# A gated cross-attention and expert kernel on one core: rank sums in a bank of their own, first expert products ahead of a permutation, stores and splits reordered

## The chip, the cores and the metric

The kernel runs on one core of a Trainium2 chip. Its engines work side by side, each through its own queue of instructions: TensorE (PE in the rows) multiplies matrices, VectorE (DVE) and ScalarE (ACT) work element by element and may read the accumulators of TensorE, GpSimd (POOL) works element by element and issues gathers, SyncE (SP) issues most other transfers. They wait for one another through semaphores that the kernel sets and awaits by hand. The metric is the device time of one execution in microseconds.

## What is computed

Two layers on 2048 tokens of width 256, in float32. A layer is a cross-attention block and a feed-forward block, each scaled by the tanh of a gate and added to its input; the first feed-forward block picks 2 of 16 experts for each token.

```python
x = x + tanh(g_xattn[0]) * L0_xattn(layernorm(x), ctx, ctx, ...)   # softmax(q k^T) v over 64 keys, by batch
x = x + tanh(g_ffn[0])   * L0_ffn(layernorm(x), gate_w, w1, w3, w2)
x = x + tanh(g_xattn[1]) * L1_xattn(layernorm(x), ctx, W, b)       # x W1^T + mean over the keys of ctx W2^T + b
x = x + tanh(g_ffn[1])   * L1_ffn(layernorm(x), ...)               # ternary weights, 256 -> 1024 -> 1024 -> 1024 -> 256

def L0_ffn(h, gate_w, w1, w3, w2):
    scores = softmax(h @ gate_w); w, idx = top_k(scores, 2); w = w / sum(w)
    y = sum over the two picked e of  w_e * (silu(h w1[e]) * (h w3[e])) w2[e]
    return y + h
```

## The kernel before

Tokens are handled in tiles of 128 and groups of four tiles: NG = 4 groups. The work has four stages. First comes a short setup. The **attention stage** (some 15 to 60 us) takes the groups one after another: transposes of X (`columns`), scores, softmax, attention (`attend`), the logits of the 16 experts, the two largest of them (`two_largest` on VectorE), and the **rank** of each token among those that picked the same expert (`ranks` on TensorE, `rank_picked` and `row_place` on VectorE). Then the **permutation**: the normed rows of all tokens (`xb`) are stored to a buffer in memory (`xb_dram`), and a product of one-hot matrices gives, for each of the NBLK = 47 blocks of 128 places, the rows to gather (`perm`); the first 16 blocks belong to experts 0 to 15, the other 31 (NREST) to whichever experts have more than 128 rows. The **block stage** (some 70 to 155 us) does for each block: gather 128 rows (GpSimd, L648), transpose them (`turns`, L1831), round to a high part (ScalarE, `high_turned`) and a low rest (VectorE, `low`), multiply with the expert's first matrices (`gate_up`, L1594 to L1596), silu and product, `down`, copy out (`yb`) and store to `ys_dram`. The last stage, four groups of the dense feed-forward network, runs from some 158 us to the end.

Every product of float32 values in the block stage uses a high and a low part of each operand. The experts' weights are loaded to six buffers ES; ScalarE writes the high part EH of an expert (`split_high`, L1363), GpSimd the low part EL of experts 0 to 12 in two halves of 384 columns (`split_low`, L587), VectorE that of experts 13 to 15 in the block stage (`expert_low`). These splits are placed in the gaps of the attention stage.

All order is written by hand. What matters here:

- On VectorE, `rank_picked(g)` (L850) waits not only for the ranks of its group but also for the logits of the next group (`pe_lg`, L856), since the ranks of group g lie in the bank of scores of group g+1.
- The last group's normed rows are made half by ScalarE (`rows_normed`, L1410), half by VectorE (`rows_normed` at L877), both from rstd and -mean*rstd, which GpSimd makes one after the other (`factors2`, L545 to L555).
- On SyncE the stores of `xb` stand behind a fill of `ys_dram` (L452), which keeps unused rows finite. GpSimd starts the gathers when `act_eh` says that all 16 EH are there (L619), both store semaphores are reached and `perm` is written.
- TensorE runs fillers (`keep_clock`, products of the identity whose result nobody reads) where it would wait.

## Time and profile before

| | us |
|---|---|
| median of 3 runs (496.54 to 498.03) | 497.9 |
| the profiled execution | 501.49 |
| its span, first to last instruction | 499.6 |
| TensorE busy | 474.8 (95%) |
| VectorE busy | 316.6 (63%) |
| ScalarE busy | 217.9 (44%) |
| GpSimd busy | 149.0 (30%) |

The profile comes from one execution and is read with the numbers of its own clock, from the span's start; some 1.9 us lie outside the span. Shares of busy time are means over stages of different kinds, so each stage is read by itself.

### The profile page before, as it was taken

Reading aid. Unit: us, or ns where it says so; the run is one execution under the profiler, and the core shown is the slowest. Engines: PE = TensorE matmul, PEld = TensorE weight load, DVE = VectorE, ACT = ScalarE, POOL = GpSimd, SP = SyncE. Lnnn points to the kernel's source line nnn. Section 1 sums busy time; section 2 is a strip of 40 time slices with the busy share of each in tenths; the row PEclk is TensorE's granted clock in tenths of the full one; section 3 lists DMA queues with packets and bytes.
Section 4 is the critical chain, followed back from the end, with each engine's and each line's share of the span. In section 5 each row is a group of like instructions: output and inputs, shape, how many; then the busy total and the mean of one; then the engine's idle time right before and its main releaser. Section 6 shows DMA issues by size and latency. Waiting matters only on the chain.

```text
span 499.6 us, 7859 instructions
## 1 busy us (share of the span) xinstructions
PE 474.8 (95%) x2760; PEld 409.5 (82%) x2760; DVE 316.6 (63%) x848; ACT 217.9 (44%) x444; POOL 149.0 (30%) x157
## 2 busy tenths in 40 slices
PE   6988979997698999999999999999999999999996
PEld 6877869997697788888978888887888898788886
DVE  2888897876675865765477766337865735554523
ACT  1679936775466966412372121336121224511110
POOL 2487857767860601110350201053110101000000
PEclk8999999999999999999999999999999999999999
DMA  8784834897653587212140420032122002022101
GB/s 285 253 284 141 284 121 142 235 315 231 203 168 114 169 288 240 76 30 77 43 128 21 106 63 2 0 101 69 43 85 64 1 1 84 15 71 69 38 2 48
DMA packets 34465, 58.82 MB, mean 118 GB/s; under 512 B 4529, under 2 KB 18353, under 8 KB 34354
## 3 DMA queue, kind: packets, MB, share of 16 engines
q1 hardware_dynamic: 29760, 47.12, 29.3%
q0 software_dynamic: 3840, 10.49, 7.3%
q10 hardware_dynamic: 818, 0.61, 0.4%
q8 instruction: 25, 0.41, 0.3%
q14 instruction: 22, 0.18, 0.1%
HBM read 47.85 MB, written 14.42 MB: 125 GB/s over the span
## 4 chain that ended last, share of the span: by engine, by line
PE 79%; DVE 7%; DMA 5%; POOL 5%; issue 2%; ACT 0%; ACTq 0%; DVEq 0%; POOLq 0%
PE bank L2017 23%; PE bank L2018 23%; PE bank L1986 6%; PE bank L1989 6%; PE bank L2050 3%; PE bank L2049 3%; PE bank L1594 2%; PE bank L1596 2%; PE bank L1595 2%; DMA xg<-xb_dram,perm 2%; POOL y_first L629 2%; POOL xg_more L648 1%; POOL xg L648 1%; DMA colv<-cols 1%; PE bank L1831 1%
## 5 line engine op out<-in xcount | busy, mean ns | idle before, releaser
L1568 ACT ACTIVATE sg<-bank,colv 128x512 f32<-128x512 f32 x64 | 44.1, 690 | 176.6 <-PE bank L2018 176.6
L2017 PE MATMUL bank<-Ah,Wr 128*128 128x512 f32 x256 | 100.2, 391 | 0.0
L2017 PE MATMUL bank<-Bh,Wr 128*128 128x512 f32 x256 | 99.9, 390 | 0.0
L2018 PE MATMUL bank<-Al,Wr 128*128 128x512 f32 x256 | 99.8, 390 | 0.0
L2018 PE MATMUL bank<-Bl,Wr 128*128 128x512 f32 x256 | 99.7, 389 | 0.0
L2017 PEld LDWEIGHTS bank<-Ah,Wr 128*128 128x128 f32 x256 | 48.1, 188 | 11.2 <-DVE Al L1281 0.8
L2018 PEld LDWEIGHTS bank<-Bl,Wr 128*128 128x128 f32 x256 | 48.1, 188 | 9.8
L2017 PEld LDWEIGHTS bank<-Bh,Wr 128*128 128x128 f32 x256 | 48.1, 188 | 9.8
L2018 PEld LDWEIGHTS bank<-Al,Wr 128*128 128x128 f32 x256 | 48.1, 188 | 9.7
L1294 DVE CAST Ah<-sg 128x512 fp32r<-128x512 f32 x32 | 13.6, 425 | 60.0 <-ACT sg L1568 60.0
L1594 PE MATMUL bank<-EL,turned 128*128 (+1 forms) x137 | 42.6, 311 | 0.3 <-ACT yb L1500 0.3
L571 POOL TENSOR_TENSOR rstd<-veps,mhalf 128x4 f32<-128x4 f32 x6 | 8.4, 1401 | 108.5 <-DVE veps L751 61.1
L1596 PE MATMUL bank<-EH,turned 128*128 (+1 forms) x137 | 38.7, 283 | 0.0
L1554 ACT ACTIVATE sg<-bank,colv 128x512 f32<-128x512 f32 x32 | 22.1, 690 | 38.1 <-PE bank L1989 37.6
L1595 PE MATMUL bank<-EH,turned 128*128 (+1 forms) x137 | 38.6, 282 | 0.0
L1277 DVE SCALAR_TENSOR_TENSOR sg<-bank,colv,sg 128x512 f32<-128x512 f32 x32 | 24.0, 751 | 22.9 <-ACT sg L1554 22.6
L1986 PE MATMUL bank<-xTh,Wr 128*128 128x512 f32 x96 | 37.7, 393 | 0.0
L1989 PE MATMUL bank<-xTl,Wr 128*128 128x512 f32 x96 | 37.6, 392 | 0.0
L1294 DVE CAST Bh<-sg 128x512 fp32r<-128x512 f32 x32 | 13.6, 425 | 37.1 <-ACT sg L1568 37.1
L648 POOL DMA_INDIRECT xg<-xb_dram,perm x32 | 31.2, 975 | 9.2 <-issue 6.8
L1096 DVE TENSOR_TENSOR turned<-bank,turned 128x384 fp32r<-128x384 f32 (+2 forms) x49 | 25.7, 525 | 9.4 <-ACT turned L1486 9.1
L1269 DVE SCALAR_TENSOR_TENSOR stage<-stage,Wr 128x512 f32<-128x512 f32 x44 | 30.1, 685 | 1.9 <-DMA stage<-panels 1.8
(294 smaller groups left out, 1024.8 us busy)
## 6 DMA issues: line engine op xcount, KB each, us to landing
Wraw<-panels SPq DMA_DIRECT2D x44, 256.0 KB, 3.8
stage<-panels SPq DMA_DIRECT2D x44, 256.0 KB, 2.6
ES<-experts SPq DMA_DIRECT2D x16, 384.0 KB, 5.2
ys_dram<-yb SPq DMA_DIRECT2D x47, 128.0 KB
ys_dram<-x SPq DMA_DIRECT2D x1, 1920.0 KB, 7.9
X<-x SPq DMA_DIRECT2D x3, 512.0 KB, 7.6
xb_dram<-xb SPq DMA_DIRECT2D x3, 512.0 KB, 5.2
out<-outb SPq DMA_DIRECT2D x3, 512.0 KB, 3.3
```

Source lines behind the costliest of these rows:

```text
L648: eng.indirect_dma_start(out=rows, out_offset=None, in_=xb_dram, in_offset=bass.IndirectOffsetOnAxis(ap=perm[:, i:i + 1], axis=0)).then_in ...
L1096: eng.tensor_tensor(low_[:, w], bank_t[b][:, w], high_[:, w].bitcast(F32), ALU.subtract).then_inc(b_xl, 1)
L1269: eng.scalar_tensor_tensor(stage[:, w % 2, :], stage[:, w % 2, :], 1.0, to.bitcast(F32), ALU.mult, ALU.not_equal, accum_out=diff[:, w:w + ...
L1294: own(eng.tensor_copy(h[0][:, m, :], sg[:, r, :]))
L1568: eng.activation(sg[:, (8 * layer + m) % 3, :], bank[m % 4][:, :], ACT.Gelu, scale=colv[:, c + m:c + m + 1]).then_inc(f_act[m], 1)
L1594: mm(dst, lhs[0], rhs[1], start=first, stop=False)
L1595: mm(dst, lhs[1], rhs[0], start=False, stop=False)
L1596: return mm(dst, lhs[0], rhs[0], start=False, stop=last)
L1986: mm(dst, w[:, u, k, :], x_high[:, k, :], start=k == 0, stop=False)
L1989: ins = mm(dst, w[:, u, k, :], x_low[:, k, :], start=False, stop=k == DK - 1 and not general)
L2017: mm(bank[m % 4][:, :], Wr[:, base:base + P], h[0][:, k, :], start=k == 0, stop=False)
L2018: ins = mm(bank[m % 4][:, :], Wr[:, base:base + P], h[1][:, k, :], start=False, stop=k == FK - 1 and not general)
```

## The change

It makes these edits, all ahead of the dense stage. An expert's whole EL has the same 768 columns before and after.

1. **Ranks in a bank of their own.** `ranks_of` gives bank 3 for every group, which `columns` also uses: `ranks(g)` begins a new sum and waits for the copies out of that bank, and `columns(3, 0)` waits for the first rank pick. `rank_picked` no longer waits for the next group's logits.
2. **Row products and context rows later.** `row_products` (for `nm1` and `w3s`) moves from group 2 to group 3 and to bank 5; `context_rows` from group 3 to behind the counts. ScalarE's copies of `nm1` and `w3s` follow the last rows.
3. **Fillers.** 0, 2, 4 and 4 ahead of the ranks of the four groups (none but 5 in the last before); fewer around the permutation.
4. **Last rows.** VectorE makes its half from mean and rstd (subtract, multiply) and so needs no -mean*rstd; the negated mean of that group moves from GpSimd to VectorE, `dve_mean`.
5. **Stores.** The fill of `ys_dram` becomes two halves, issued behind the loads of experts 10 and 11; VectorE's half of the last rows is stored ahead of ScalarE's.
6. **Splits.** EL in quarters of 192 columns (EL_CUT 4); expert 12 moves from ahead of the gathers to behind gather 4 (LOW_AT). On ScalarE, EH of two experts fewer in group 2, and of experts 13 to 15 last, behind the exponential `ex`.
7. **First products ahead of the permutation of the rest.** A third pair of first buffers; `low(0)` and `low(1)` stand inside VectorE's chain that leads to `ohb`, the one-hot matrix of the other 31 blocks; the experts of these blocks (`experts_of_blocks`) come after `low(2)`; on TensorE the permutation stands behind the second `gate_up`.

```diff
-EL_CUT = 2
+EL_CUT = 4
+RANK_FILLERS = (0, 2, 4, 4)
+FILL_AT = (10, 11)
+LOW_AT = 4
...
         def ranks_of(g):
-            first = TG * SC + (TG * E if g == NG - 1 else 0)
-            return bank[(g + 1) % 2][:, first:first + TG * E]
+            return bank_ranks[:, 0:TG * E]
...
             store_rows(1, 0, TG)
-            eng.dma_start(ys_dram[E * P:T * TOPK, :], x[0:T * TOPK - E * P, :]).then_inc(dma_fill, 16)
             store_rows(2, 0, TG)
-            store_rows(NG - 1, 0, 2)
             eng.wait_ge(dve_xb, 2)
             eng.dma_start(xb_tiles[:, NT - 2:NT, :], xb[:, 1, 2:TG, :]).then_inc(dma_xb[1], 16)
+            store_rows(NG - 1, 0, 2)
...
             def split_low(n):
                 w = EXP_COLS // EL_CUT
+                n = n * EL_CUT // 2
...
+                if i == LOW_AT:
+                    split_low(2)
...
                 eng.wait_ge(pe_rank, g + 1)
-                if g + 1 < NG:
-                    eng.wait_ge(pe_lg, g + 2)
...
-                if g == 2:
-                    eng.wait_ge(pe_setup, PE_LATE)
-                    eng.activation(nm1[:, :], bank[3][:, 0:D], ACT.Copy, scale=-1.0 / D).then_inc(act_setup, 1)
-                    eng.activation(w3s[:, :], bank[3][:, D:2 * D], ACT.Copy, scale=tg[:, 3:4]).then_inc(act_setup, 1)
                 if g < NG - 1:
-                    split_high(3)
+                    split_high(3 if g < NG - 2 else 1)
             rows_normed(NG - 1, 0, 2)
-            split_high(E)
+            split_high(1)
+            eng.wait_ge(pe_setup, PE_LATE)
...
             turns(0)
+            keep_clock(bank[1], 3)
             turns(1)
-            permutation(bank_y[0][:, 0:NREST], lambda r, t: ohb[:, r, :, t], rest_there)
             for i in range(NBLK + DOWN):
                 expert_there(i)
                 if i < 2:
                     gate_up(i, offsets[i])
+                    if i == 1:
+                        permutation(bank_y[0][:, 0:NREST], lambda r, t: ohb[:, r, :, t], rest_there)
                     turns(i + 2)
```

Three places show how the queues change. In each row stand the line of its kernel, the operation, what it writes and reads, and a count. ScalarE from the last group's attention copy to its first work on blocks, before:

```order
L1392 ACTIVATE X<-bank 128x512 x2
L1410 ACTIVATE xb<-X,nmr_78,rstd_77 128x256 x4
L1399 ACTIVATE ohr<-ohr,tok_125 128x256 x4
L1410 ACTIVATE xb<-X,nmr_78,rstd_77 128x256 x2
L1363 ACTIVATE EH<-ES 128x768 x2
L1477 ACTIVATE crow<-bank,tg 128x512
L1479 ACTIVATE ex<-ld 128x16
L1503 ACT_TABLE_LOAD
L1503 ACTIVATE unused<-ones 1x1
L1486 ACTIVATE first_high_189<-bank 128x256
```

and now:

```order
L1409 ACTIVATE X<-bank 128x512 x2
L1427 ACTIVATE xb<-X,nmr_78,rstd_77 128x256 x4
L1416 ACTIVATE ohr<-ohr,tok_125 128x256 x4
L1427 ACTIVATE xb<-X,nmr_78,rstd_77 128x256 x2
L1380 ACTIVATE EH<-ES 128x768
L1490 ACTIVATE nm_115<-bank 128x256
L1491 ACTIVATE w3s<-bank,tg 128x256
L1493 ACTIVATE crow<-bank,tg 128x512
L1495 ACTIVATE ex<-ld 128x16
L1380 ACTIVATE EH<-ES 128x768 x3
L1519 ACT_TABLE_LOAD
```

Three EH stand behind `ex`, which stood last before, and ahead of them the two late copies.

GpSimd from the last group's splits to the seventh gather (the two ISA rows clear semaphores), before:

```order
L587 TENSOR_TENSOR EL<-ES,EH 128x384 x2
L615 DMA xg_more<-x,ix_134 128x256
L620 ISA x2
L648 DMA xg_more<-xb_dram,perm 128x256
L648 DMA xg<-xb_dram,perm 128x256 x4
L648 DMA xg_more<-xb_dram,perm 128x256 x2
```

and now:

```order
L628 DMA xg_more<-x,ix_134 128x256
L633 ISA x2
L661 DMA xg_more<-xb_dram,perm 128x256
L661 DMA xg<-xb_dram,perm 128x256 x4
L601 TENSOR_TENSOR EL<-ES,EH 128x192 x4
L661 DMA xg_more<-xb_dram,perm 128x256 x2
```

The split of expert 12 stood ahead of the first gather and stands between gathers 4 and 5.

VectorE where the blocks' one-hot matrix `ohb` is made (`sba`, `sbm`, `pblk` and `pslot` lead to it, `first_low` is `low(0)` and `low(1)`, `bexp` begins the experts of the blocks), before:

```order
L1010 TENSOR_TENSOR sba<-sba,pb_142 128x512
L1012 TENSOR_TENSOR sbm<-eq,sba 128x512
L1014 TENSOR_REDUCE pblk<-sbm 128x32
L1015 SCALAR_TENSOR_TENSOR pslot<-ixf,rnk 128x32
L1017 SCALAR_TENSOR_TENSOR pblk<-rnk,pblk 128x32
L1019 TENSOR_TENSOR pslot<-pslot,pblk 128x32
L1021 TENSOR_TENSOR pblk_143<-pslot,pos 128x4x2x4
L1027 TENSOR_TENSOR ohb<-kbrep,pblk_143 128x496 x2
L1096 TENSOR_TENSOR first_low_191<-bank,first_high_189 128x256
L1158 TENSOR_SCALAR bexp<-pinc_163,kc 128x16
```

and now:

```order
L1031 TENSOR_TENSOR sba<-sba,pb_142 128x512
L1020 TENSOR_TENSOR first_low_192<-bank,first_high_189 128x256
L1034 TENSOR_TENSOR sbm<-eq,sba 128x512
L1036 TENSOR_REDUCE pblk<-sbm 128x32
L1037 SCALAR_TENSOR_TENSOR pslot<-ixf,rnk 128x32
L1020 TENSOR_TENSOR first_low_193<-bank,first_high_190 128x256
L1040 SCALAR_TENSOR_TENSOR pblk<-rnk,pblk 128x32
L1042 TENSOR_TENSOR pslot<-pslot,pblk 128x32
L1044 TENSOR_TENSOR pblk_143<-pslot,pos 128x4x2x4
L1050 TENSOR_TENSOR ohb<-kbrep,pblk_143 128x496 x2
L1135 TENSOR_TENSOR bh<-bank,bsg 128x128
L1020 TENSOR_TENSOR first_low_194<-bank,first_high_191 128x256
```

Two subtractions that need gathered rows stand ahead of `ohb`, and the first block's product and the third `low` follow it at once.

## Rows read from the trace of the kernel before

**Rows 1.** The page's chain that ended last: shares by engine.

```profile
PE 79%; DVE 7%; DMA 5%; POOL 5%; issue 2%; ACT 0%; ACTq 0%; DVEq 0%; POOLq 0%
```

**Rows 2.** Chain in time, 47 to 71 us: start, us, engine, line.

```profile
47.60 0.86 PE bank L1722 x4
...
58.00 1.33 DVE stats L775 x4
...
61.80 2.09 DVE xb L883 x2
...
63.90 4.48 DMA xb_dram<-xb
...
69.15 0.96 POOL xg_more L648
```

**Rows 3.** VectorE groups, 31 to 58 us: count, busy, mean ns, idle before, releaser.

```profile
L857 DVE TENSOR_TENSOR rtmp<-eq,bank 128x128 f32<-128x128 f16 x3 | 0.9, 288 | 2.7 <-PE bank L1671 2.7
```

**Rows 4.** Timeline, 40 to 62 us: start, us, engine, operation, [idle before <-releaser].

```profile
45.35 2.30 ACT L1363 ACTIVATE EH<-ES 128x768 fp32r<-128x768 f32 x3
...
47.83 0.35 ACT L1370 ACTIVATE pr<-pr,nmx 128x64 f32<-128x64 f32 x1 [0.19 <-DVE nmx L820]
...
56.99 1.07 ACT L1392 ACTIVATE X<-bank 128x512 f32<-128x512 f32 x2
...
60.14 0.23 POOL L551 TENSOR_SCALAR mean<-mv 128x4 f32<-128x4 f32 x1
...
61.56 0.20 POOL L555 TENSOR_TENSOR nmr<-mean,rstd 128x4 f32<-128x4 f32 x1
```

**Rows 5.** GpSimd groups, 20 to 70 us, shapes apart.

```profile
L587 POOL TENSOR_TENSOR EL<-ES,EH 128x384 fp32r<-128x384 f32 x24 | 23.9, 1019 | 5.1 <-DVE pr L827 3.6 <-DVE both L848 0.7 <-ACT EH L1363 0.6
L550 POOL TENSOR_SCALAR veps<-mv 128x4 f32<-128x4 f32 x4 | 0.9, 233 | 0.9 <-DVE mv L778 0.7
```

**Rows 6.** Issues of the last store alone (63.8 to 64.2 us), then the one before it (62.8 to 63.3).

```profile
xb_dram<-xb SPq DMA_DIRECT2D x1, 256.0 KB, 4.5
```

```profile
xb_dram<-xb SPq DMA_DIRECT2D x1, 256.0 KB, 2.9
```

**Rows 7.** Timeline, 62 to 82 us.

```profile
66.04 0.22 ACT L1479 ACTIVATE ex<-ld 128x16 f32<-128x16 f32 x1 [1.11 <-DVE ld L965]
...
70.10 0.42 DVE L1012 TENSOR_TENSOR sbm<-eq,sba 128x512 f16<-128x512 f16 x1
...
71.97 0.44 PE L1831 MATMUL bank<-ident,xg_more 128*128 128x128 f32 x2 [0.42 <-DMA xg_more<-xb_dram,perm]
...
72.05 0.74 DVE L1027 TENSOR_TENSOR ohb<-kbrep,pblk 128x496 f16<-128x496 f16 x2
...
72.86 0.42 DVE L1096 TENSOR_TENSOR first_low<-bank,first_high 128x256 fp32r<-128x256 f32 x1
...
74.60 0.15 DVE L1173 TENSOR_REDUCE end<-count 1x1 f32<-1x17 f32 x1
...
75.42 0.95 POOL L648 DMA_INDIRECT xg_more<-xb_dram,perm  x1 [0.30 <-issue]
...
78.61 0.38 PE L1831 MATMUL bank<-ident,xg_more 128*128 128x128 f32 x2
```

**Rows 8.** Timeline of TensorE, 8 to 110 us: the start, the fillers, the transposes of block 13.

```profile
8.32 2.08 PE L1609 MATMUL bank<-ctxTs,WkT 128*128 128x128 f32 x8 [2.73 <-DMA colv<-cols]
```

```profile
69.08 2.47 PE L1601 MATMUL bank<-ident 128*128 128x128 f32 x20 [0.95 <-POOLq L652]
```

```profile
90.14 0.41 PE L1831 MATMUL bank<-ident,xg 128*128 128x128 f32 x2 [0.49 <-DMA xg<-xb_dram,perm]
```

**Rows 9.** Windows of one us, TensorE: length, busy, granted clock, DMA share, GB/s.

```profile
8.00:9.00 1.00, 0.68 (x3) 0.52 0.99 356
...
14.00:15.00 1.00, 1.00 (x7) 0.57 1.11 356
15.00:16.00 1.00, 1.00 (x9) 1.00 1.10 348
```

More of the change, by code:

```diff
@@ L280, in flamingo_kernel @@
         put = over(route_end, e_off)
-        first_high, first_low = ([put(f"{n}{b}", [P, DK * P], F32R) for b in range(2)] for n in ("first_high", "first_low"))
+        FIRST = 3
+        first_high, first_low = ([put(f"{n}{b}", [P, DK * P], F32R) for b in range(FIRST)] for n in ("first_high", "first_low"))
         outb = nc.alloc_sbuf_tensor_at("outb", [P, TG, D], F32, offset=bl_off)
@@ L344, in flamingo_kernel @@
         bank_y, bank_first = [bank[6], bank[5]], bank[7]
+        bank_ranks, bank_places, bank_late = bank[3], bank[1], bank[5]
         def turned_pair(n):
-            return (first_high[n], first_low[n]) if n < 2 else (t_high[n % 3], t_low[n % 3])
+            return (first_high[n], first_low[n]) if n < FIRST else (t_high[n % 3], t_low[n % 3])
         def joint(n):
@@ L447, in _ @@
                     eng.dma_start(ys_dram[T * TOPK:NBLK * P, :], x[0:NBLK * P - T * TOPK, :]).then_inc(dma_fill, 16)
+                if e in FILL_AT:
+                    n = T * TOPK - E * P
+                    a, b = (n * (FILL_AT.index(e) + k) // len(FILL_AT) for k in range(2))
+                    eng.dma_start(ys_dram[E * P + a:E * P + b, :], x[a:b, :]).then_inc(dma_fill, 16)
                 if e == 12:
@@ L974, in _ @@
             eng.wait_ge(pe_perm, 1)
-            permuted(bank[3], slice(0, E))
+            permuted(bank_places, slice(0, E))
             eng.wait_ge(pe_rank, NG + 1)
@@ L1000, in _, with low @@
             own(eng.tensor_tensor(pd16[:, :], prest_0[:, :], prest[:, :], ALU.subtract))
+            def low(n):
+                b, w = n % 3, joint(n)
+                high_, low_ = turned_pair(n)
+                eng.wait_ge(b_xh, n + 1)
+                eng.tensor_tensor(low_[:, w], bank_t[b][:, w], high_[:, w].bitcast(F32), ALU.subtract).then_inc(b_xl, 1)
             flat = "p g r t -> p (g r t)"
@@ L1011, in _ @@
             own.done()
+            low(0)
             own(eng.tensor_tensor(sb, eq[:, :, :, :, :].rearrange("p g r t e -> p (g r t) e"), sa, ALU.mult))
@@ L1016, in _ @@
             own.done()
+            low(1)
             own(eng.scalar_tensor_tensor(pblk[:, :], rank, float(P), pblk[:, :], ALU.is_ge, ALU.mult))
@@ L1185, in _ @@
                 if i == 0:
+                    experts_of_blocks()
                     eng.wait_ge(pe_perm, 2)
@@ L1618, in columns @@
                     eng.wait_ge(act_xT, DK * (g - 1) + (1 if g < 3 else DK))
+                if k == 0 and g > 2:
+                    eng.wait_ge(dve_rk, g - 2)
                 if k == 1 and g >= 2:
@@ L1770, in _ @@
                 else:
-                    keep_clock(bank[2], 5)
+                    row_products()
+                keep_clock(bank[2], RANK_FILLERS[g])
                 ranks(g)
@@ L1888, in part1_half @@
                 ins.then_inc(n_p1, 1)
-            keep_clock(bank[5], 9)
+            keep_clock(bank[0], 4)
             eng.wait_ge(act_setup, ACT_LATE + 2)
```

78 lines of the change are left out of this document (38 added, 40 removed).

## The prediction

> **What bounds the kernel now.** The chain that ended last is TensorE for 79%, and most of it lies in the dense stage, which this change doesn't touch [rows 1]. So I looked only at what decides when the block stage begins and how fast its first blocks run, and followed the chain in time there [rows 2]. In the attention stage it goes through VectorE and, in group 2, through TensorE with the row products in it. Then the last group's statistics (58.00), the root on GpSimd, VectorE's two last rows (61.80 to 63.89), their store (63.90, 4.48 us to landing) and the first gather at 69.15 follow in single file. Call the last of these G. From G, GpSimd issues a gather every 1.25 us (gather 5 at 75.42), and TensorE transposes block 0 at 71.97, 2.82 us behind it, and block 5 at 78.61, G + 9.46 [rows 7]. From there the blocks take 1.44 us each (8 of them to 90.14, one wait among them [rows 7, 8]), bound by TensorE. So two numbers decide: how much earlier G comes, and how far block 5 then stands behind G. What is gained at block 5 is carried to the end, unless a wait further on eats it.
>
> **The rank picks.** VectorE waited three times, 2.7 us together, at the rank pick of groups 0 to 2, each time until the next group's logits were done [rows 3]. The ranks themselves stood ready. The new bank takes this wait away; what ends last there is then VectorE's own statistics. The new wait of `columns(3, 0)` for the first rank pick costs nothing: those transposes start some 2 us after it. Nor does the wait of `ranks(g)` for the copies out of bank 3, the last of which ended before `both` did. The 2.7 us don't all arrive. ScalarE rounds three EH in a row from 45.35 to 47.65, and the softmax of group 3 follows after only 0.19 us of idle time [rows 4]. Group 1 gives VectorE 1.4 us by then (of two picks), the softmax only 0.8 to 0.9, for it now queues behind the EH. By the end of the third pick I carry the sum forward row by row: 2.0 us, no more. For this to reach the last statistics their X must be there: ScalarE's copy started at 56.99 [rows 4], and with the attention sums 0.9 us earlier and two EH (1.5 us) and the two late copies (0.8 us) out of its queue, it starts near 54.4 and ends at 55.5, ahead of the 56.0 at which VectorE wants it.
>
> **The row products and fillers.** The products at 47.60 were on the chain with some 1.5 us [rows 2] and stand now behind the last attention product; there they and 4 fillers cost TensorE 2.6 us (20 filler rows, that is 10 fillers, took 2.47 us [rows 8], a quarter each) between 53.8 and 56.4. The last ranks then end near 57.2, half a microsecond before VectorE asks. In groups 1 and 2 the fillers (0.5 and 1.0 us) end as `both` or the softmax weights arrive. All these I take as hidden. If the cover of the last were gone, 4 fillers would cost up to 1.0 us.
>
> **The last rows.** GpSimd loses the negated mean (0.23 and a gap) and VectorE no longer waits for nmr (0.20 and gaps) [rows 4]: 0.59 us. VectorE's own rank work (1.35 us behind the statistics) and the new mean then end last, so 0.45 of it counts. VectorE's last rows begin at 61.80 - 2.0 - 0.45 = 59.35, against 61.80 [rows 2].
>
> **GpSimd's splits.** A half of 384 columns takes 1.02 us in the mean with contention and 0.97 alone, 24 of them 23.9 us [rows 5]; an operation on 4 columns takes 0.23. If all of the time goes with the columns, a quarter takes 0.49; if 0.2 of it is fixed, 0.60. A larger fixed part would not fit the half. I take 0.50, since a split of 512 would then follow the same line, and keep 0.60 for the range. GpSimd had 1.4 us of idle time around the last group's splits (0.7 and 0.7 [rows 5]); with its start 1.0 us earlier and the same work it is ready at 57.5, just in time for the statistics at 57.8. At 0.60, 12 quarters make it 1.2 us later, and the gain shrinks by 0.6 to 0.9. The Trainium skill, GPSIMD Engine Reference, section Elementwise — side-by-side cycle accounting, gives a two-input operation about 2.6 cycles an element plus a dispatch for each instruction; by its figures a quarter would be an estimated 0.42 us and the dispatch, and the sum would not move. Its dispatch cost speaks against finer splits, and this trace can't show it at 192 columns.
>
> **G itself.** Before, G came 7.35 us behind the start of the last rows: the store landed at +6.6. Its 256 KB took 4.5 us, the one before it 2.9 [rows 6]; a 1.9 MB fill issued at 53 us and three stores shared the rings. With the fill gone from there I expect 2.9 to 4.5 for the new last store, which now is ScalarE's and is issued some 0.6 us behind VectorE's, at +2.7: landed at +5.6 to +7.2. But another wait takes its place. GpSimd also waits for all EH, and the last three now stand behind `ex`, which ran 4.24 us behind the start of the last rows (66.04 against 61.80) [rows 2, 7]. With 0.22 for itself and 2.3 for three EH [rows 4] they end at +6.75. Then come clearing two semaphores and the issue, 0.8 us. G is at 59.35 + 7.55 = 66.9, 2.25 us earlier. The Trainium skill, DMA: Bandwidth & Descriptors, section Anatomy of one DMA, gives about 2.0 us and the bytes over 436 GB/s. By it the last store would take an estimated 2.6 us and be well ahead of the EH; the rows show 2.9 to 4.5, and G is the same by both.
>
> **The first blocks.** Here the gain is given back, in two ways of equal size that overlap. First, VectorE. It reached `sbm` 8.3 us behind the start of the last rows (70.10 against 61.80), so it will be there at 67.65; now it must first do `low(0)`, which needs the first rows turned and rounded: 72.86 - 69.15 = G + 3.7, or 70.6 [rows 2, 7]. It waits some 3 us. Then low 0.42, `sbm` 0.42, the reduction and `pslot` 0.9, low(1) 0.42, three small operations 0.65, `ohb` 0.74 [rows 7]: G + 7.4, where `ohb` was done at G + 3.64. The permutation ends near G + 9.0 behind it. VectorE goes on with a product and `low(2)` (0.7) and the blocks' experts (1.5, from the end of low(0) to 74.75 [rows 7]) to G + 9.6. TensorE waits for these before its small product (0.2), then the transposes of block 4 (0.65), the products of block 2 (0.8), and block 5 comes at G + 11.35: 1.9 us further behind G than now. Second, GpSimd: gather 5 was issued at 75.42, G + 6.27 [rows 7]; four quarters (2.0 to 2.4) in front make it G + 8.3 to 8.7, and with 2.82 us to its transposes block 5 can't start before G + 11.1 to 11.5. The later of the two counts, not the sum: G + 11.35. Taking the products out of the way of the permutation thus buys nothing in this program, for the permutation's own inputs wait for them on VectorE.
>
> **The sum.** Block 5 comes at 66.9 + 11.35 = 78.25 instead of 78.61: 0.35 us earlier. Further on, gather 13 had 4.3 us to landing and TensorE waited for it [rows 8]; that gather is issued 0.3 us earlier too. The end of the run moves with it: 501.49 - 0.35 = 501.1 for a profiled execution. The profiled execution lies 3.6 us above the median of the runs, 497.9; I put the same difference there: **497.5**. A measurement of this kernel tells 0.3%, about 1.5 us, from no change, so this is no change.
>
> **Rivals.**
> *The gain is kept* (0.24). G comes 2.25 us earlier, and the blocks don't give it back. For: the block loop had waits of its own (0.49 us and some issue time at block 13 [rows 8]) that an earlier or more even start could absorb, and a landing faster than 2.82 us with the stores out of the way pulls both terms. Against: both terms of 1.9 us are built from operations that must be done in this order. 497.9 - 2.25 = 495.7.
> *GpSimd's fixed part* (0.13). Quarters at 0.60: G is only 1.5 us earlier, gather 5 at G + 8.7, block 5 at G + 11.5, so 78.61 + 0.5; with the fillers' cover gone as well, 1.0 us more. 498.4 to 499.4. It decides from a quarter of 0.57 on.
> *TensorE's clock falls* (0.15), the one that ends on the other side. At the start TensorE sat idle for 2.73 us [rows 8], and the granted clock was then half, the 1.2 GHz level, from 8 until past 14 us [rows 9]; everywhere else it is 1.00. Ahead of G TensorE now has 5 + 4 fillers in place of 8 + 9, ends them near 64.9 and waits until G, 66.9: 2.0 us in one piece, against 0.95 before [rows 8]. If the clock falls there, ten fillers ahead of block 0 take 4.9 us instead of 2.47 and end 2.1 us behind the first rows, and the work after it runs at half pace for some 4 us more, of which VectorE's waits hide about half: 2.9 us in all. 497.5 + 2.9 = 500.4. It decides from an idle piece somewhere between 0.95 and 2.73 us. The Trainium skill, TensorE: Matmul & The Clock Gate, section The HAM clock gate, says that an idle stretch takes the clock to half; the trace agrees at 8 us, and whether 2.0 us is enough no row shows.
> *The forecast* (0.48), with 496.6 to 498.6 as its own range: G by 0.8 us either way, the landing at block 13 by 0.6.
>
> **How the numbers follow.** Range 495.4 to 499.4: it takes in the kept gain and the fixed part, and leaves out the clock and the far ends. Faster by over 0.3%: the kept gain, and a little of the forecast's lower end, 0.27. Slower by over 0.3%: the clock, 0.15, and a little of the fixed part, 0.17. Same: 0.56.
>
> **What would show it.** In the profile after: no wait at the rank pick for logits; last rows on VectorE starting near 59.4 (at 60 or later, GpSimd's quarters or ScalarE's queue are at fault); the first gather near 66.9 and released by ScalarE's EH, not by the store; a wait of some 3 us on VectorE at `low(0)`; `ohb` done 7.4 us behind G; block 5 transposed 11.35 us behind it; the granted clock 1.00 from 60 us on. If block 5 stands under G + 10, the giving back is wrong and the time is that of the first rival.

## The result, and the profile after

The changed kernel takes **500.07 us** in the median (498.09 to 504.62, 17 runs), beside 497.75 us of the kernel before (494.98 to 500.37, 17 runs): a ratio of 1.0055, with a 95% interval of 1.0037 to 1.0074. It is slower by over 0.3%. Ratios and their intervals, here and below, leave out single runs of more than 1.5% above the fastest of their kernel; medians are of all its runs. The forecast of 497.5 us is 2.6 us off, and 500.07 lies outside its range. Run again beside other kernels it gave 1.0056 (1.0023 to 1.0089).

The profiled execution took 500.31 us, with a span of 498.4. The two profiles differ in their start: the kernel before lost time at half clock there [rows 9], the changed one did not. So both are read from one point behind that, the first of the maxima that VectorE takes of the router's logits (L838 before, L853 after; call it A), and from G, the first gather from `xb_dram`. All places are in us; "last rows" are VectorE's two of the last group, and a block stands where TensorE begins to transpose it.

| | A | last rows start | G | block 5 transposed | block 12 |
|---|---|---|---|---|---|
| before | 28.08 | A + 33.72 | A + 41.07 | G + 9.46 | A + 60.02 |
| changed | 24.41 | A + 33.60 | A + 40.18 | G + 13.63 | A + 64.14 |

The rows behind the table, of the kernel before (A alone) and of the changed one (A, last rows, G, block 5), in order of time (start, length in us, engine, line, operation, operands, count, idle time before and its releaser):

```profile
28.08 0.42 DVE L838 MAX8 m<-bank 128x8 f32<-128x16 f32 x4
```

```profile
24.41 0.42 DVE L853 MAX8 m<-bank 128x8 f32<-128x16 f32 x4
58.01 0.74 DVE L898 TENSOR_SCALAR xb<-X,mv,rstd 128x256 f32<-128x256 f32 x2 [0.85 <-POOL rstd L564]
64.59 1.07 POOL L661 DMA_INDIRECT xg_more<-xb_dram,perm  x1 [4.63 <-ACT EH L1380]
78.22 0.63 PE L1846 MATMUL bank<-ident,xg_more 128*128 128x128 f32 x2
```

The chain of waits of the changed kernel, in order of time (start, length, what), shows where the path went. Before, it ran through VectorE and TensorE in the attention stage [rows 2]; now a good part of it is GpSimd's splits:

```profile
46.87 3.34 POOL EL L601 x6
50.73 1.06 POOL mean L562
53.73 2.79 POOL EL L601 x5
58.28 1.09 ACT xb L1427 x2
61.42 2.21 ACT EH L1380 x3
64.59 2.88 DMA xg_more<-xb_dram,perm
```

The last two rows are as forecast: G is released by ScalarE's EH. The first three, all of GpSimd, are not. Between A and the last rows VectorE and GpSimd are both busier than before. These are the busy times from A to the last rows (stretch and its length; then for PE, PEld, DVE, ACT, POOL busy time and count; granted clock, DMA share, GB/s), before and changed:

```profile
28.10:61.80 33.70, 30.68 (x238) 25.13 (x237) 28.76 (x133) 30.08 (x77) 26.72 (x36) 1.00 0.66 218
```

```profile
24.50:58.00 33.50, 30.24 (x232) 25.26 (x231) 31.25 (x132) 28.32 (x72) 31.05 (x53) 1.00 0.69 234
```

VectorE's three waits [rows 3] are gone, and its busy time has grown by 2.5 us for very nearly the same operations. Behind G, VectorE, GpSimd and TensorE show this (`pslot` and `pblk` are the small slot operations that lead to the one-hots `ohb`):

```profile
68.48 0.42 DVE L1020 TENSOR_TENSOR first_low<-bank,first_high 128x256 fp32r<-128x256 f32 x1 [3.64 <-ACT first_high L1502]
70.75 1.69 DVE L1042 TENSOR_TENSOR pslot<-pslot,pblk 128x32 f32<-128x32 f32 x1
73.01 0.74 DVE L1050 TENSOR_TENSOR ohb<-kbrep,pblk 128x496 f16<-128x496 f16 x2
70.69 2.23 POOL L601 TENSOR_TENSOR EL<-ES,EH 128x192 fp32r<-128x192 f32 x4
64.53 2.47 PE L1617 MATMUL bank<-ident 128*128 128x128 f32 x20 [2.69 <-POOLq L665]
73.58 2.06 PE L1810 MATMUL bank<-ohb,ohr 128*128 128x31 f16 x32 [1.97 <-DVE ohb L1050]
```

The wait at `low(0)` is there. A slot operation on 32 columns takes 1.69 us beside GpSimd's four quarters. In the kernel before the same one took 0.19:

```profile
71.60 0.19 DVE L1019 TENSOR_TENSOR pslot<-pslot,pblk 128x32 f32<-128x32 f32 x1
```

TensorE is idle for 2.69 us ahead of G and for 1.97 us ahead of the second permutation. And its granted clock falls to the lower level (same columns as above):

```profile
60.00:70.00 10.00, 6.36 (x54) 5.41 (x51) 5.91 (x29) 5.87 (x12) 4.19 (x5) 1.00 0.32 94
72.00:74.00 2.00, 0.42 (x8) 0.45 (x9) 1.93 (x6) 0.00 (x0) 1.84 (x3) 0.83 0.00 0
74.00:80.00 6.00, 6.00 (x50) 5.56 (x48) 4.44 (x20) 1.65 (x4) 4.48 (x6) 0.50 0.30 92
80.00:90.00 10.00, 10.00 (x87) 10.00 (x87) 8.04 (x24) 7.56 (x21) 7.87 (x8) 0.99 0.54 157
```

The clock fell a second time, from 117.7 to 121.1 us, right behind a wait of 2.56 us for a gather. In the kernel before it stood at full speed there. First the changed kernel, then the kernel before:

```profile
117.00:121.00 4.00, 3.33 (x16) 3.36 (x17) 3.23 (x11) 1.15 (x3) 3.08 (x4) 0.58 0.47 145
```

```profile
117.00:121.00 4.00, 3.36 (x28) 3.21 (x28) 3.26 (x11) 2.20 (x7) 3.09 (x4) 1.00 0.59 170
```

Not all of what is lost by block 12 reaches the end. Block 12 stands 4.1 us later behind A than before, and the end of the span 2.4 us later (A + 473.97 against A + 471.55). By block 18 the difference is down to 3.0 us, 0.65 of it at block 13, where the kernel before waits for its gather [rows 8] and the changed one does not. That is what the first rival had in mind. A second profile of the changed kernel (below) has 4.2 us at block 12 and 3.3 at the end, so the part behind block 12 is not settled.

Three suspects follow, and a fourth for the missing gain: the clock (C), GpSimd's quarters between gathers (L), the order of the first products (O), and GpSimd's splits in the attention stage, by their size (Q) or by their mere presence (W).

### The profile page after: what moved, and what is told of

The parts are those of the page before. It is cut to its first block, busy times and chain, and to the rows that moved or that the text cites. A ratio compares the mean times of both kernels' runs of the same rounds, so it can differ in the third digit from the quotient of the medians.

```text
span 498.4 us, 7866 instructions
## 1 busy us (share of the span) xinstructions
PE 474.6 (95%) x2748; PEld 409.1 (82%) x2748; DVE 319.0 (64%) x849; ACT 217.9 (44%) x444; POOL 154.4 (31%) x182
## 4 chain that ended last, share of the span: by engine, by line
PE 78%; DVE 10%; POOL 4%; DMA 3%; issue 2%; ACT 2%; SPq 0%; POOLq 0%; DVEq 0%
PE bank L2034 23%; PE bank L2035 23%; PE bank L2003 6%; PE bank L2006 6%; PE bank L2067 3%; PE bank L2066 3%; PE bank L1610 3%; PE bank L1612 3%; PE bank L1611 3%; PE bank L1846 2%; POOL EL L601 1%; DVE stats L778 1%; DMA gw<-gate 1%; POOL y_first L642 1%; DMA y_first<-ys_dram,slots 1%
## 5 line engine op out<-in xcount | busy, mean ns | idle before, releaser
L2067 PE MATMUL bank<-Wr,Al 128*128 128x256 f32 x128 | 30.9, 283 | 0.0
```

Source lines behind the costliest of these rows:

```text
L2067: ins = mm(dst, hA[1][:, k, j * P:(j + 1) * P], w, start=False, stop=k == FK - 1)
```

## The experiments

The runs came in five groups, each on its own chip, with 12 runs of each kernel unless said otherwise. On three of these chips (the first, fourth and fifth group) the kernel before took 513.8, 515.4 and 513.3 us instead of 497.7 and 498.0. So ratios are compared within a group, or between groups of the same kind.

### One part at a time (kernel before: 513.8 us)

**More fillers ahead of G.**

```
-            keep_clock(bank[0], 4)
+            keep_clock(bank[0], 14)
```

> Changed kernel with 14 fillers in place of 4 ahead of TensorE's wait for the first gather (10 x 0.25 us put into an idle piece of 2.69 us). Theory C (the clock falls because of that idle piece, and that is most of the loss): the granted clock stays 1.00 from 60 to 80 us, block 5 is transposed 2 to 3 us earlier behind the first gather (G + 11 instead of G + 13.6), ratio to the kernel before 0.999 to 1.001. Rival P (the clock falls because of TensorE's later wait of 1.97 us for the one-hots of the second permutation): the clock still falls at 72 us, ratio unchanged near 1.0055. Rival Q (the loss is GpSimd's quarters): ratio 1.004 or more with the clock at 1.00.

Ratio 1.0011 (0.9988 to 1.0033). The idle piece shrank to 0.44 us and the clock stayed up until 76 us. Then it fell for nearly 7 us, behind waits of 1.04 us, 0.60 us and, for the one-hots, 1.55 us. Filling the first piece alone thus did not keep the clock up, and block 5 still stood at G + 13.5: C's forecast of G + 11 was wrong.

**Halves.** `EL_CUT = 4` to `EL_CUT = 2`.

> Changed kernel with halves of 384 columns in place of quarters of 192, everything else as it is. Theory Q (quarters cost GpSimd more for each element and keep its port busy, which slows VectorE's small operations in the attention stage): last rows on VectorE start 1.5 to 2.4 us earlier against the first maximum of the stage, the first gather too, ratio 1.001 to 1.003 if the rest is kept. Theory C (clock alone): the last rows start no earlier, ratio 1.0055 as for the changed kernel, or more, since the idle piece ahead of the gather stays.

Ratio 1.0021 (0.9987 to 1.0055). The last rows start at A + 33.14, 0.5 to 0.6 us earlier than with quarters, not 1.5 to 2.4. So the size of the pieces is the smaller part. The slot operation was held even longer; these are VectorE and GpSimd of this run:

```profile
70.29 2.21 DVE L1037 SCALAR_TENSOR_TENSOR pslot<-ixf,rnk 128x32 f32<-128x32 f32 x1
70.50 1.95 POOL L601 TENSOR_TENSOR EL<-ES,EH 128x384 fp32r<-128x384 f32 x2
```

**The last expert's quarters back ahead of the gathers.**

```
                 factors2(g)
+            split_low(2)
...
-                if i == LOW_AT:
-                    split_low(2)
```

> Changed kernel with the last expert's four quarters on GpSimd put back ahead of the gathers (2.2 us that fit into GpSimd's wait for ScalarE's splits). Theory L (the quarters between gathers 4 and 5 delay gather 5 by 2.2 us and slow VectorE's slot operation from 0.19 to 1.69 us): the slot operation takes 0.2 us again, the one-hots are done near G + 7.7 instead of G + 9.2, TensorE waits 0.5 us for them instead of 1.97, block 5 at G + 11.4 to 12, ratio 1.001 to 1.003. Rival C (the clock falls through the idle piece ahead of the first gather): the clock falls all the same, and ratio 1.004 or more. Should the clock stay up with that idle piece as it was, the 1.97 us wait was its cause.

Ratio 1.0027 (0.9992 to 1.0061). The slot operation took 0.18 us again and the one-hots started at G + 7.35. But G came 7.34 us behind the start of the last rows instead of 6.58, TensorE stopped three times within the permutation, 2.7 us together, with nothing in the profile to wait for, and the clock was down twice before 81 us. Block 5 came at G + 15.8 and not at the 11.4 to 12 of L. Inconclusive for the time, clear for the slot operation.

**The second permutation first.** The permutation, `low(0)`, `low(1)` and `experts_of_blocks()` back where the kernel before has them.

> Changed kernel with the second permutation, the first roundings and the experts of the blocks back in the order of the kernel before, GpSimd's quarters still between gathers 4 and 5. Theory O (the first products ahead of the permutation are what gives the gain back, for VectorE's one-hots wait for the first rows): one-hots done by G + 4, no wait of TensorE for them, block 5 at G + 11.3 by gather 5 alone, ratio 1.001 to 1.002 and less if the clock stays up. Theory L (gather 5 alone decides) and theory C (the idle piece): block 5 stays at G + 13 or so and ratio 1.004 or more.

Ratio 1.0023 (0.9994 to 1.0052). The one-hots started at G + 2.25 and no engine waited for them. Block 5 came at G + 12.47 with gather 5 at G + 8.73, and the clock was at half from 64 to 70 us. The quarters now held up another small operation, again until about three of the four were done:

```profile
71.01 1.79 DVE L1054 TENSOR_TENSOR ends<-count,prest 1x16 f32<-1x16 f32 x1
71.07 2.24 POOL L601 TENSOR_TENSOR EL<-ES,EH 128x192 fp32r<-128x192 f32 x4
```

All four intervals hold 1.0; none of the parts can be told from another by its time here. Of the forecasts, O's of the one-hots (by G + 4) came true, and its block 5 at G + 11.3 did not.

### The clock, the sum of all, and the last rows (kernel before: 497.66 us)

**The changed kernel again.**

> The changed kernel as it is, for a comparison with the others on one chip. Theories C, Q, L and O alike: near 1.0055 where block 12 is late by 3 us as in its profile above. If later waits of this chip absorb an early loss (rival A: on a chip whose gathered rows and stored blocks come later, what was lost at block 5 disappears in the waits around blocks 28 to 32), the ratio is 1.000 to 1.003 and all variants lie close together.

Ratio 1.0056 (1.0023 to 1.0089), block 12 at A + 64.20. Rival A does not hold on this chip. For the first group's, where the changed kernel itself did not run, it stays open.

**Fillers in both idle pieces.** As in the first run, and

```
                     if i == 1:
+                        keep_clock(bank[5], 8)
                         permutation(bank_y[0][:, 0:NREST], lambda r, t: ohb[:, r, :, t], rest_there)
```

> Changed kernel with 14 fillers in place of 4 ahead of the wait for the first gather, and 8 fillers ahead of the second permutation, where TensorE waits 1.5 to 2 us for VectorE's one-hots. Theory C in its wider form (either idle piece of 1.5 us and more lets the clock fall some 8 us later): the granted clock is 1.00 from 60 to 85 us, block 6 comes 1.5 to 2.5 us earlier behind the first gather, and the ratio is 0.003 to 0.005 below that of the changed kernel run beside it. Rival: the clock is at 1.00 and the ratio the same as the changed kernel's within 0.001, since the blocks wait for gathers and VectorE anyway.

Ratio 1.0038 (1.0009 to 1.0067), 0.0018 or 0.9 us below the run before it, less than C expected, and with intervals that overlap. The clock is up throughout, and block 12 comes at A + 62.32 instead of 64.20:

```profile
72.00:74.00 2.00, 2.00 (x27) 1.99 (x26) 1.93 (x8) 0.00 (x0) 1.54 (x3) 1.00 0.00 0
74.00:80.00 6.00, 6.00 (x64) 5.77 (x62) 5.57 (x22) 3.27 (x9) 4.78 (x5) 1.00 0.30 91
```

So with the clock up block 12 is 1.9 us earlier, 1.6 of it behind G (from G + 23.86 to G + 22.30); the other 0.3 us stands ahead of G, where the clock was the same. The clock did not fall near 117 us in this run either. Further waits for gathers (1.36 us at 100.5, among others) take a part of that back. By the ratios, the larger part of the loss is not the clock.

**Everything suspected taken out.** Halves, 14 fillers, the second permutation first as above, 12 experts on GpSimd (`POOL_EL = 12`; VectorE splits the thirteenth in the block stage), and on ScalarE

```
-            split_high(1)
+            split_high(E)
             eng.wait_ge(pe_setup, PE_LATE)
...
             eng.activation(ex[:, :], ld[:, :], ACT.Exp).then_inc(act_ex, 1)
-            split_high(E)
```

> Changed kernel with every suspected cost taken out: halves in place of quarters, expert 12 split by VectorE in the block stage in place of GpSimd between the gathers, the second permutation and the experts of the blocks in the order of the kernel before, 14 fillers ahead of the first gather, and ScalarE's last three splits ahead of its three small copies. Theory: last rows on VectorE 1 to 2 us earlier than in the changed kernel, first gather 1 us earlier behind them (limited by the store of ScalarE's rows), block 5 at G + 9.5: 3 to 5 us below the kernel before, ratio 0.990 to 0.994. Rival A (later waits absorb it): block 12 early, ratio 0.998 to 1.000 all the same.

Ratio 0.998 (0.9939 to 1.002); 496.41 us. G is at A + 38.45 and block 12 at A + 58.74, but its last rows start only at A + 33.17. The attention stage thus has gained half a microsecond at most, although the wait is gone and no quarter is left, and the total misses the forecast 0.990 to 0.994. Block 12 is 1.3 us earlier than in the kernel before, the end of the span behind A 0.8 us, and the median 1.25 us below, so no large gain is absorbed later; the interval, 4 us wide, can't tell more.

**The kernel before, with 12 experts on GpSimd.** `POOL_EL = 13` to `POOL_EL = 12`, nothing else.

> Kernel before with one number changed: GpSimd splits 12 experts instead of 13, VectorE the thirteenth in the block stage. Theory S (VectorE's last two rows took 2.08 us instead of 0.74 because GpSimd split two halves in exactly these 2.01 us; one engine holds the other up): the last rows take 0.74 us, their store starts 1.3 us earlier, the first gather and block 5 too, ratio 0.997. Rival (they took 2.08 us because they are multiply and add with two scalars, not subtract and multiply): they still take 2.08 us, ratio 1.000.

Ratio 1.0015 (0.9984 to 1.0046). Theory S holds for the operation: the same two rows, in the same form, take 0.79 us instead of the 2.09 of [rows 2].

```profile
57.83 0.79 DVE L883 TENSOR_SCALAR xb<-X,rstd,nmr 128x256 f32<-128x256 f32 x2 [0.81 <-POOL nmr L555]
70.00:74.00 4.00, 4.00 (x27) 3.56 (x25) 1.42 (x6) 1.21 (x4) 2.93 (x4) 0.59 0.36 105
```

G moved 1.1 us to A + 39.95. But the clock fell at 70 us, behind idle pieces of 1.15, 0.49 and 0.75 us, and block 12 came at A + 60.73, 0.7 us later than in the kernel before. S's forecast for the time, 0.997, lies outside the interval.

### Where the wait went, and the order of the first blocks (kernel before: 497.98 us)

**10 experts on GpSimd.** The combined kernel, and

```
-POOL_EL = 12
+POOL_EL = 10
...
             low(1)
+            expert_low(POOL_EL)
...
-                if 2 <= i < 2 + E - POOL_EL:
-                    expert_low(POOL_EL + i - 2)
+                if 1 <= i < E - POOL_EL:
+                    expert_low(POOL_EL + i)
```

> The combined kernel with 10 experts split by GpSimd in place of 12; VectorE splits the other two in the block stage too. GpSimd has then no split left in the attention stage's group 3 and few in group 2. Theory W (the wait taken from VectorE turned into longer operations, because an operation that meets a split on GpSimd is held up until that ends): in groups 2 and 3 VectorE's small operations fall back to 0.17 to 0.30 us, its busy time from the first maximum to the last rows falls from 33.2 us by 1 to 2 us, and the last rows start at 31.3 to 32.2 us behind the first maximum, in place of 33.2. Rival: VectorE's busy time stays at 33 us. The total is a side matter: 0.995 to 1.000 by how much VectorE's additional splits (0.95 us each) delay the first blocks.

**Ratio 0.9923** (0.9893 to 0.9953), 495.92 us, 7 runs. The last rows start at A + 31.31, 1.9 us earlier than in the combined kernel, and VectorE's busy time up to them falls from 31.61 to 29.65 us. W's forecasts hold, except that `eq` still takes 0.98 us in group 2, beside a split, and that the total lies below its 0.995.

**The combined kernel with the wait put back.**

```
                 eng.wait_ge(pe_rank, g + 1)
+                if g + 1 < NG:
+                    eng.wait_ge(pe_lg, g + 2)
```

> The combined kernel with the wait of the rank pick for the next group's logits put back (the ranks stay in their own bank). Theory W (that wait cost nothing, for without it VectorE only runs into GpSimd's splits): VectorE's idle time returns (2.7 us), its busy time falls by as much, and the last rows start within 0.3 us of where the combined kernel has them, 33.2 us behind the first maximum; ratio within 0.001 of the combined kernel's 0.998. Rival (the wait was worth something in the end): last rows 1 to 2 us later, ratio 1.000 to 1.002.

Ratio 0.9995 (0.9962 to 1.0028). The last rows start at A + 33.14, against 33.17 without the wait (on another chip of the same kind). This is the decisive pair. The changed kernel itself was not run with the wait. First the combined kernel's busy times from A to the last rows, then that of the kernel with the wait, and its list of waits (line, releaser, sum, times, longest):

```profile
24.10:57.30 33.20, 29.24 (x227) 24.44 (x226) 31.61 (x134) 28.13 (x72) 27.49 (x33) 1.00 0.68 240
```

```profile
24.50:57.70 33.20, 29.54 (x227) 24.49 (x226) 28.92 (x134) 27.97 (x72) 26.25 (x33) 1.00 0.69 236
DVE rtmp L871 <- PE bank L1690: 2.7, 3, 1.0
```

VectorE's 2.7 us of idle time and 2.7 us more of busy time (31.61 - 28.92) are the same time. What fills it can be seen operation by operation. These are VectorE and GpSimd of the combined kernel in group 1:

```profile
35.43 1.03 DVE L860 TENSOR_TENSOR eq<-kc,ixf 128x128 f16<-128x128 f32 x1
37.16 1.40 DVE L790 BATCH_NORM_STATS2 stats<-X 128x6 f32<-128x256 f32 x4
39.49 0.77 DVE L879 TENSOR_SCALAR first<-rnk 128x8 bf16<-128x8 f32 x1
35.31 1.01 POOL L601 TENSOR_TENSOR EL<-ES,EH 128x384 fp32r<-128x384 f32 x1
37.32 2.92 POOL L601 TENSOR_TENSOR EL<-ES,EH 128x384 fp32r<-128x384 f32 x3 [1.00 <-DVE pr L842]
```

and these the same two of VectorE with the wait:

```profile
36.08 0.78 DVE L858 CAST ixf<-ix 128x8 f32<-128x8 uint32 x1
36.90 0.29 DVE L860 TENSOR_TENSOR eq<-kc,ixf 128x128 f16<-128x128 f32 x1
41.22 0.17 DVE L881 TENSOR_SCALAR first<-rnk 128x8 bf16<-128x8 f32 x1
```

Without the wait `eq` lasts until just behind the end of GpSimd's half at 36.32, and `first` until the third half ends at 40.24. The statistics, nearly all of them inside GpSimd's run, take 1.40 us in both kernels. With the wait, VectorE sits idle for 0.89 us up to 40.58, over a part of GpSimd's run, reads the bank, and `first` comes behind the run at its own length. `eq` must be read together with the cast ahead of it. With the wait the cast is the one that is held, 0.78 us for 0.17, and `eq` is not, so that this place makes only 0.1 us of difference. Over the four groups, without the wait against with it, `eq` takes 2.1 us more, `first` 0.9, `ohf` 0.8 and `both` 0.7, and the cast 1.4 less. In the two kernels together `eq` takes 0.29 us in the three groups in which no split stands beside it, and 0.97 to 1.04 in the five in which one does.

**12 experts on GpSimd in the changed kernel.** `POOL_EL = 13` to `POOL_EL = 12`: no quarters between the gathers.

> The changed kernel with 12 experts split by GpSimd in place of 13: the four quarters between gathers 4 and 5 are gone, VectorE splits that expert in the block stage. Theory L (these quarters hold up VectorE's slot operations by 1.3 to 1.5 us and gather 5 by 2.2 us): the one-hots start at G + 7.0, TensorE waits under 1 us for them, gather 5 at G + 6.3, block 5 at G + 11.3 to 12 in place of 13.6, ratio 1.002 to 1.004 in place of 1.0056. Rival O (the order of the first products alone gives the gain back): ratio 1.005 or more.

Ratio 1.0019 (0.999 to 1.0047). One-hots at G + 7.15, gather 5 at G + 6.40, block 5 at G + 12.31, later than L had it, for the clock was down at 64 and again at 74 us.

**And the second permutation first.**

> As the run before, and the second permutation, the first roundings and the experts of the blocks in the order of the kernel before. Theory O (waiting for the first rows in the middle of the one-hots' chain costs a further 1.5 to 2 us): one-hots start at G + 3 or earlier, no wait of TensorE for them, block 5 at G + 9.5 to 11; ratio 0.999 to 1.001 in place of 1.002 to 1.004, part of it hanging on whether the clock falls ahead of the first gather, where the idle piece of 2.7 us is left as it is. Rival L (the quarters were all): the same as the run before within 0.001.

Ratio 0.9982 (0.9957 to 1.0006), block 5 at G + 9.64. Beside the G + 9.46 of [rows 7], the giving back is gone. TensorE's row ahead of G and its clock, first of the run with the products first, then of this one:

```profile
64.52 3.85 PE L1617 MATMUL bank<-ident 128*128 128x128 f32 x20 [2.68 <-POOLq L665]
64.00:66.00 2.00, 1.48 (x7) 1.51 (x8) 0.79 (x2) 1.11 (x2) 1.11 (x2) 0.50 0.00 0
```

```profile
64.45 2.47 PE L1617 MATMUL bank<-ident 128*128 128x128 f32 x20 [2.69 <-POOLq L665]
64.00:66.00 2.00, 1.55 (x14) 1.58 (x15) 1.90 (x5) 1.04 (x2) 1.17 (x2) 1.00 0.00 0
```

The idle pieces are equal, 2.68 and 2.69 us. After one of them the clock was down, after the other it was not.

### Does the wait have a price at all (kernel before: 515.4 and 513.3 us)

**10 experts again.**

> The kernel with 10 experts split by GpSimd once more, beside the next three: 0.990 to 0.995 as before, last rows at 31.3 us behind the first maximum.

Ratio 0.9948 (0.9917 to 0.998). Its profile cannot be compared: TensorE was at half clock after 22 us, VectorE waited 1.6 us for it, and the last rows came at A + 32.60.

**10 experts, with the wait.**

> The kernel with 10 experts on GpSimd, with the wait of the rank pick for the next group's logits put back. Theory W (the wait cost nothing only because GpSimd's splits stood behind it): with those splits mostly gone its price shows, last rows 0.8 to 1.8 us later (32.1 to 33.1 us behind the first maximum in place of 31.3), ratio 0.002 to 0.004 above the run before it. Rival (ranks and logits come in the same order anyway, the wait never had a price): last rows at 31.3 to 31.6, ratio within 0.001.

Ratio 0.9984 (0.9944 to 1.0024), last rows at A + 32.46.

**The kernel before with 10 experts on GpSimd.**

> The kernel before with 10 experts split by GpSimd in place of 13 and nothing else changed. If the rank bank is worth nothing at all, this is as good as the kernels with it: ratio 0.993. By theory W it keeps its three waits (2.7 us), the last rows start at 33.2 to 33.7 us behind the first maximum and take 0.74 us, the first gather comes 1 to 1.5 us earlier, and the ratio is 0.997 to 1.000, at the upper end if the clock falls in the idle pieces around the first gather as it did with 12 experts.

Ratio 1.0005 (0.9974 to 1.0036): no gain, just above W's 0.997 to 1.000, and the 0.993 expected of a bank that is worth nothing lies outside the interval. In the kernel before, taking the splits away is worth nothing that shows; in the combined kernel the wait taken away was worth nothing with 12 experts. Last rows at A + 33.53; the store behind them took 4.51 us to landing and set G at A + 40.33.

**The same with 14 fillers for 9.**

> As the run before, with 14 fillers in place of 9 ahead of TensorE's wait for the first gather, whose idle piece was 1.15 us with 12 experts. Theory C (idle pieces around the first gather let the clock fall in part of the executions): granted clock 1.00 from 66 to 80 us, 0.5 to 2 us below the run before it, ratio 0.995 to 0.998. Rival: no difference.

Ratio 1.0019 (0.9976 to 1.0062): no gain either, where 0.995 to 0.998 was expected. The store took 5.84 us in this profile, so that 1.92 us of idle time stood ahead of G all the same, and the clock was down from 72 to 82 us. It says nothing on C.

**10 experts without and with the wait, on one chip.**

> The kernel with 10 experts split by GpSimd a third time, since the profile of its second run shows TensorE at half clock from 22 to 28 us and VectorE waiting 1.6 us for it. Without that: last rows 31.3 us behind the first maximum, VectorE without idle time, ratio 0.991 to 0.995.

> The same with the wait of the rank pick put back. Theory W: three waits, 2.7 us together, of which the last rows come 0.8 to 1.4 us later than in the run before (32.1 to 32.7 us behind the first maximum), ratio 0.002 to 0.004 above it. Rival (the wait never had a price): last rows within 0.3 us, ratio within 0.001.

Ratios 0.9953 (0.9924 to 0.9981) and 0.9971 (0.9942 to 1.0001); last rows at A + 31.35 and at A + 32.47. The busy times up to the last rows, without and with:

```profile
23.90:55.30 31.40, 28.54 (x225) 24.17 (x224) 29.75 (x134) 28.06 (x72) 22.83 (x29) 1.00 0.70 242
```

```profile
23.80:56.20 32.40, 29.50 (x227) 24.38 (x225) 28.05 (x133) 28.04 (x72) 22.16 (x29) 1.00 0.70 242
DVE rtmp L871 <- PE bank L1691: 2.7, 3, 1.0
```

So the wait does have a price, 1.1 us of its 2.7, once a part of GpSimd's splits is out of the way; with 12 experts it had none. That the times differ by 0.0018 is in line with it, but the intervals overlap.

## Why the prediction was wrong

**Where the miss lies.** Block 5 was to come 0.35 us earlier and came 3.3 us later (A + 53.81 for A + 50.53). Of these 3.6 us, 1.35 are G, which gained 0.9 us and not 2.25, and 2.3 are the first blocks, which gave back 4.2 us and not 1.9. Behind the first and behind more than half of the second stands the same thing: the sum never let a split of GpSimd lengthen an operation of VectorE. The clock is the rest of the second.

**The rank picks: this is the step that failed first.** I took VectorE's 2.7 us of waiting for time to be had, and carried 2.0 us to the last statistics. 0.1 us arrived (A + 33.72 to A + 33.60, and 33.75 in the second profile), and that with 0.45 us of the last rows' step in it: on the time scale of the kernel before they start at 28.08 + 33.60 = 61.68, where I had 59.35. The sum asked whose result each engine waits for, and never what VectorE's next operations meet. They met GpSimd's splits, which had run beside the idle time. The run with the wait put back shows the exchange, 2.7 for 2.7; the runs with 10 experts show what comes when the splits go. The Trainium skill, SBUF — State Buffer, section Who interferes with whom, has the rule that speaks against this step: a VectorE instruction with two inputs in SBUF, or in a mode that uses both its ports, contends with a GpSimd instruction that reads SBUF, and the loser is blocked fully. By that rule `eq` and `ohf`, with two inputs, are held, `first` and the cast can be, and the statistics and all that read a bank are not. The trace agrees: `eq` 1.03 us beside a half and 0.29 clear of one, the four statistics 1.40 us either way.

**GpSimd's splits: mis-sized by 0.06 us each, and mis-placed.** I took 0.50 for a quarter and 0.60 as the bound, from one size of split alone, which can't tell a fixed part. Six in a row take 3.34 us, 0.557 each; the 38 between A and the last rows average 0.599, for GpSimd is held up by VectorE in turn. GpSimd was busy 31.05 of 33.50 us, and VectorE waited 0.85 us for its root, where I had it just in time. By the runs with halves this is worth 0.45 to 0.6 us. The rival that rested on 0.60 and decided from 0.57 had the right place, but not this price.

**The last rows.** I kept their 2.09 us [rows 2] and should not have: two halves of GpSimd stood beside them, and moving these behind the gathers gave back 1.35 us. Most of what G gained comes from there.

**G itself.** The mechanism was right: released by ScalarE's EH, the store not in the way. G came 6.58 us behind the start of the last rows, where I had 7.55. The shorter last rows make 1.35 us of difference, of which 0.3 is lost again because `ex` stood behind ScalarE's late copies (its input was done at 60.83, it started at 61.21). The last store landed at +3.8 (issued at 59.40, 2.45 us), not at +5.6 to +7.2, which changed nothing, for the EH came later. (The fill that I put at 1.9 MB is 2.1 MB by its line, 2048 rows of 1 KB; the sum doesn't use it.) In all G gained 0.9 us and not 2.25.

**The first blocks: right in kind, 1.9 us forecast and 4.2 us measured.** The wait at `low(0)` was 3.64 us (I had 3). The one-hots should have been done at G + 7.4 and were at G + 9.2, for a slot operation was held for 1.5 us and its neighbour for 0.3 us by the quarters. I had counted the quarters on GpSimd's own queue alone. The clock gave the rest: with it up, block 5 stands at G + 12.77; with the quarters gone too the one-hots start at G + 7.15; and with the permutation first block 5 is at G + 9.64.

**The clock, the rival at 0.15.** It fell, and the time is near the 500.4 of that rival. That is no credit to it. Its price was 1.6 us at block 12 and about 0.9 us at the end, not 2.9, and it came in the second idle piece, at 73 us, which that rival did not have. The length of the idle piece alone doesn't decide either: 2.68 us brought the clock down and 2.69 us did not.

**The sum.** With the ratios of the runs on chips of one kind: 1.0056; without the quarters between the gathers 1.0019; with the permutation first as well 0.9982. Either step is about 1.8 us, uncertain by some 2 us, so that the sum is firm and its split is not. What is left, 0.9982, is in line with the 0.9 us that G gained, though its interval holds 1.

**A version that beats the kernel before**, and by the ratios of the chips of one kind the changed one too: the changed kernel with halves, 10 experts on GpSimd, more fillers ahead of G, ScalarE's splits ahead of its copies, and the first blocks in the order of the kernel before. 0.9923, 0.9948 and 0.9953 in three groups, none of whose intervals reaches 1.

## What to carry to other kernels

An idle piece is worth its length only if the operations that move into it keep their duration there: look at what the engine that can hold them up does in that stretch, and price a held operation at the time until that engine's operation ends at least, and at the worst until its run of operations ends. Where an operation's duration in the trace is well above that of its like elsewhere (2.09 against 0.74 us here), ask who ran beside it before carrying it into a sum. And count a moved operation on every engine that it can hold up, not on its own queue alone.

## What the runs showed of the hardware

- A VectorE operation that meets a row of GpSimd splits can be held for more than one of them: 2.21 us for 32 columns while two halves ran (to 72.50 and 72.45), 1.69 us over three of four quarters. It is not always so: the two operations of [rows 2] took 1.07 and 1.09 us beside two halves, one half each. GpSimd is held in the same way: its mean on 4 columns (50.73 to 51.78) took 1.06 us, where [rows 5] have 0.23 for such an operation, while VectorE's `ohr`, with two inputs, ran to 51.70.
- A quarter of 192 columns takes 0.557 us and a half of 384 columns 0.974 (three in 2.92), so by these two sizes an estimated 0.14 us of each do not go with the columns.
- The granted clock after equal idle pieces differs between two executions (above), of kernels that are alike up to there. In the changed kernel the piece of 2.69 us left it at 1.00 for 8 us, and it fell in the course of the second piece, of 1.97 us.
- On the three chips on which the kernel before takes 513 to 515 us, TensorE stops in the middle of the second permutation with nothing to wait for, in several kernels; here in the one with 10 experts. On the other chips the same 32 products run in one piece of 2.06 us. I haven't found the cause.

```profile
65.70 1.70 PE L1810 MATMUL bank<-ohb,ohr 128*128 128x31 f16 x26
69.26 0.28 PE L1810 MATMUL bank<-ohb,ohr 128*128 128x31 f16 x2 [1.14 <-issue]
70.69 0.28 PE L1810 MATMUL bank<-ohb,ohr 128*128 128x31 f16 x2 [1.15 <-issue]
```
